# A language-model tower on one core: probabilities transposed during the last sequence, experts' tokens found in groups of three

## The reference

```python
combined = concat([_ngram_embed(byte_sequence, t, n) for t, n in zip(tables, (2, 3, 4))])
h = einsum('bsk,dk->bsd', combined, proj_w) + proj_b
# attention on layernorm(h): branches "cross" (keys from a stride-2 convolution), "dot" and "cosine",
# each softmax(q k^T) v and a layer norm; a 3-way softmax gate mixes the branches; h += z
x2 = layernorm(h)
Sm = softmax(x2 @ W_router + b_router)        # 8192 tokens x 32 experts
G, idx = top_k(Sm.T, 256)                     # each expert's 256 best tokens, ties to the lowest token
act = silu(x2[idx] @ W_up[group] + b_up)      # 4 experts share one W_up
y.at[idx].add(G * (act @ W_down[expert] + b_down))
return h + y
```

## Time and profile before

| | us |
|---|---|
| median of three runs | 1395.65 (1395.10 to 1399.89) |
| the profiled execution | 1398.12 |
| its span, first to last instruction | 1395.9 |
| PE / DVE / ACT / POOL busy | 1111.2 / 841.5 / 673.8 / 799.9 |
| first block | 0 to 1055.6 |
| threshold (30 steps) | 1060.5 to 1123.9 |
| masks and token lists until the first gather | 1123.95 to 1160.6 |
| first gather to first scatter | 1160.6 to 1187.0 |
| experts, first scatter to the end | 1187.0 to 1395.9 |

### The profile page before, as it was taken

One profiled execution on the slowest core, in us unless ns is written; L12 is line 12 of the kernel. 1 busy time (PEld: TensorE's weight loads), 2 busy tenths in 40 slices (PEclk: granted clock), 3 DMA queues, 4 the chain that ended last, 5 costly groups with the idle time before them and its releaser, 6 DMA issues. The chain is left out here.

```text
span 1395.9 us, 22815 instructions
## 1 busy us (share of the span) xinstructions
PE 1111.2 (80%) x7389; PEld 970.8 (70%) x7390; DVE 841.5 (60%) x2493; ACT 673.8 (48%) x1690; POOL 799.9 (57%) x1257
## 2 busy tenths in 40 slices
PE   4569999999999999999999999999953235666572
PEld 3459788888978878888887888788852124555462
DVE  4235677777676867767776777776756875111110
ACT  0335666656565655665565566555534515212110
POOL 5355676667467657747755864545550002788875
PEclk9979999999999999999999999999985556888877
DMA  2010000000001101001010100000001000444442
GB/s 93 16 29 20 16 26 29 22 26 27 9 24 29 30 13 39 24 9 30 23 30 22 31 22 9 17 11 9 18 17 51 0 0 19 78 80 82 82 75 28
DMA packets 49080, 42.45 MB, mean 30 GB/s; under 512 B 6728, under 2 KB 44488, under 8 KB 48840
## 3 DMA queue, kind: packets, MB, share of 16 engines
q0 software_dynamic: 18432, 22.04, 8.0%
q1 hardware_dynamic: 30536, 19.00, 4.5%
HBM read 27.38 MB, written 13.63 MB: 29 GB/s over the span
## 5 line engine op out<-in xcount | busy, mean ns | idle before, releaser
L595 PE MATMUL mixed<-v,pT 128*128 128x132 f32 x2560 | 324.5, 279 | 5.2 <-issue 4.8
L595 PEld LDWEIGHTS mixed<-v,pT 128*128 128x128 f32 x2560 | 307.3, 193 | 5.6 <-issue 5.6
L1046 POOL DMA_INDIRECT gram<-in_emb,ids x192 | 191.3, 997 | 75.0 <-issue 51.7
L827 DVE TENSOR_REDUCE neg_max<-scores 128x1 f32<-128x1024 f32 (+1 forms) x192 | 199.1, 1037 | 51.9 <-PE scores L408 50.0
L975 ACT ACTIVATE probs<-scores,neg_max 128x1024 f32<-128x1024 f32 (+1 forms) x192 | 186.5, 971 | 59.9 <-DVE neg_max L827 59.8
L984 ACT ACTIVATE pT<-turned 128x512 f32<-128x512 f32 x214 | 127.4, 595 | 65.4 <-PE turned L576 62.0
L576 PE MATMUL turned<-con,probs 128*128 128x128 f32 x856 | 128.0, 277 | 30.3 <-ACT probs L975 12.1
L1088 POOL TENSOR_TENSOR zb<-row,gate 128x384 f32<-128x384 f32 x64 | 54.6, 853 | 157.5 <-DVE gate L865 156.6
L406 PE MATMUL scores<-k_hi,q_hi 128*128 128x512 f32 x320 | 136.0, 425 | 1.9 <-DVE q_lo L730 1.9
L1650 POOL DMA_INDIRECT xg<-token_table,slots x64 | 63.8, 997 | 121.1 <-DVE slots L1533 101.9
L576 PEld LDWEIGHTS turned<-con,probs 128*128 128x128 f32 x856 | 99.3, 142 | 47.5 <-ACT probs L975 19.8
(11 more groups left out here) (335 smaller groups left out, 2422.1 us busy)
## 6 DMA issues: line engine op xcount, KB each, us to landing
wd<-in_w_down SPq DMA_DIRECT2D x32, 171.0 KB
token_table<-w SPq DMA_DIRECT2D x16, 320.0 KB
out_h<-h SPq DMA_DIRECT2D x16, 256.0 KB, 2.3
gram<-in_emb,ids POOLq DMA_INDIRECT x192
wu<-in_w_up SPq DMA_DIRECT2D x8, 170.5 KB
w<-in_weights SPq DMA_DIRECT2D x1, 1174.0 KB, 6.6
xg<-token_table,slots POOLq DMA_INDIRECT x64
out_h<-yw,slots POOLq DMA_INDIRECT x64
```

The lines of the kernel that those rows point to most:

```text
L595: last = pe.matmul(mixed[:, 0:VW], pT[:, n % 2, j * P:(j + 1) * P], vals, start=(j == 0), stop=(last_half and j == half * 4 + 3))
L827: dve.tensor_reduce(neg_max[:, n % 4:n % 4 + 1], scores[:, (n % 2) * S:(n % 2) * S + width], AX_X, ALU.max, negate=True).then_inc(maxed, 1)
L1046: pool.indirect_dma_start(gram[:, t % 4, g, :], None, emb[g], bass.IndirectOffsetOnAxis(ap=ids[:, s, t, g:g + 1], axis=0)).then_inc(gather ...
```

## The change

1. The shared banks are no longer handed out in turn: a small table of times (a unit is 4.9 long, users begin at 1.5, 2.2, 2.6 or 4.8 in it and hold a bank 2.7 or 1.7) picks the bank that comes free first.
2. In the last sequence the probabilities of the first six sequences are transposed as items in units 4, 6 and 8 (`probT0` to `probT2`, four blocks of four tiles each, one sequence being two blocks), those of the next three blocks in the tail (`probT3`); only the last block is transposed in the second block. The storage order of `prob` becomes that of the tiles.
3. The last tile is routed alone (`x2T2`, `route2`), the three ahead of it together. `prob` is written ahead of `trow`.
4. The stores to HBM are awaited by POOL ahead of its first gather, not by SP at the end of the first block. The bit tables are loaded in the first block.
5. The masks are made in four groups of eight experts. The rank of a tie is summed in PSUM by matmuls (`sums`, `places`) and compared with 256 in one DVE operation (`choose`), in place of the scan over all.
6. The token lists are found three experts at a time (`rank`, `rows_before`, `rows`, `reach`, `find_rows`). Two triples come before the first expert, the other nine stand inside the loop over experts, one in each of its first nine rounds.
7. For that the banks are divided anew: `up` has one bank pair and `down` one bank, no longer two by turns. Four experts are gathered ahead instead of three.

```diff
+UNIT_LONG = 4.9
+USED_AT = dict(first=1.5, half0=2.2, half1=2.6, second=4.8)
+HELD = dict(item=2.7, half=1.7)
...
-        _ring = (_ring + 1) % 3
+        _ring = min(range(3), key=lambda j: _free[j])
+        _start = max(_s * UNIT_LONG + USED_AT[_where], _free[_ring])
+        _free[_ring] = _start + HELD["item" if isinstance(_user, int) else "half"]
...
+LAST = tuple(line + extra for line, extra in zip(STEADY, ("",) * 4 + (" probT0", "", " probT1", "", " probT2") + ("",) * 15))
+DRAIN = ("|", "|", "|", "probT3- |", "|", "x2T1- |", "route1- |", "|", "x2T2- |", "route2- |")
...
-            for half in range(2):
-                sp.wait_ge(h1_stored[half], 16 * B)
-                sp.wait_ge(row_stored[half], 16 * B)
...
+            def probT_item(j, dst):
+                blocks = range(j * 4, min(j * 4 + 4, TT // CHUNKS - 1))
+                last_half = blocks[-1]
+                pe.wait_ge(route_v, (last_half + 1) * 5)
+                for i, u in enumerate(blocks):
+                    last = pe.transpose(dst[:, i * P:(i + 1) * P],
+                                        prob[:, u * CHUNKS:(u + 1) * CHUNKS, :].rearrange("p c e -> p (c e)"), ident)
...
-        for u in range(CT):
-            last = pe.transpose(scores[:, u * P:(u + 1) * P], prob[:, u * CHUNKS:(u + 1) * CHUNKS, :].rearrange("p c e -> p (c e)"), ident)
+        pe.transpose(scores[:, 0:P], prob[:, (CT - 1) * CHUNKS:CT * CHUNKS, :].rearrange("p c e -> p (c e)"), ident
+                     ).then_inc(prob_turned, 1)
...
+        def sums(g):
+            if g >= 1:
+                pe.wait_ge(sums_a, g)
+            pe.wait_ge(over_ok, g + 1)
+            for j in range(GE):
+                pe.matmul(down_bank[0:TT, j:j + 1], over[:, :, g * GE + j], ones_bf[:, 0:1], start=True, stop=True)
+            if g >= 2:
+                pe.wait_ge(chosen_ok, g - 1)
+            pe.matmul(place_bank(g), far_down[:], over[:, :, g * GE:(g + 1) * GE], start=True, stop=False)
+            pe.wait_ge(tie_ok, g + 1)
+            for j in range(GE):
+                last = pe.matmul(down_bank[0:TT, GE + j:GE + j + 1], tie[:, :, g * GE + j], ones_bf[:, 0:1],
+                                 start=True, stop=True)
+            last.then_inc(sums_t, 1)
+            pe.matmul(place_bank(g), upto_bf[:], tie[:, :, g * GE:(g + 1) * GE], start=False, stop=False)
+
+        def places(g):
+            pe.wait_ge(sums_a, g + 1)
+            pe.matmul(place_bank(g), ones_bf[0:TT, :], tile_sums[:, g, 0, :].unsqueeze(1).to_broadcast([TT, TT, GE]),
+                      start=False, stop=False)
+            pe.wait_ge(ties_ok, g + 1)
+            pe.matmul(place_bank(g), ones_bf[0:TT, :], ties_before[:, g, :, :], start=False, stop=True).then_inc(place_t, 1)
...
         def up(e):
             pe.wait_ge(xt_v, e + 1)
-            if e >= 2:
-                pe.wait_ge(hid_a, e - 1)
+            if e >= 1:
+                pe.wait_ge(hid_a, e)
...
         def down(e):
             pe.wait_ge(hid_a, e + 1)
-            if e >= 2:
-                pe.wait_ge(y_v, e - 1)
+            if e >= 1:
+                pe.wait_ge(y_v, e)
...
+        pe.wait_ge(chosen_ok, GROUPS)
         up(0)
         turn(1)
         for e in range(NE):
+            g = e + FIRST_TRIPLES
+            if g < len(TRIPLES):
+                rank(g)
             if e + 1 < NE:
                 up(e + 1)
+            if g < len(TRIPLES):
+                rows_before(g)
             down(e)
+            if g < len(TRIPLES):
+                rows(g)
             if e + 2 < NE:
                 turn(e + 2)
...
-        dve.tensor_scalar(thr_row[:], thr_row[:], cand[0:NE, :].bitcast(F32), None, ALU.add).then_inc(thr_v, 1)
-        everywhere = thr[:].unsqueeze(1).to_broadcast([P, CT, NE])
-        for mask, op in ((over, ALU.is_gt), (tie, ALU.is_equal)):
-            for c in range(CHUNKS):
-                last = dve.tensor_tensor(mask[:, c * CT:(c + 1) * CT, :], prob[:, c:TT:CHUNKS, :], everywhere, op)
...
-        dve.tensor_tensor_scan(tie_before[:].rearrange("p e t -> p (e t)"), keep[:].rearrange("p e t -> p (e t)"),
...
-        dve.tensor_tensor(chosen[:, 1:TT + 1, :], tie_in[:], over[:], ALU.add).then_inc(chosen_ok, 1)
...
+        def choose(g):
+            at = slice(g * GE, (g + 1) * GE)
+            if g == 0:
+                dve.wait_ge(made_g, 1)
+            dve.wait_ge(reach_ok, g + 1)
+            dve.wait_ge(place_t, g + 1)
+            dve.scalar_tensor_tensor(out=chosen[:, 1:TT + 1, at], in0=place_bank(g).rearrange("p (t e) -> p t e", e=GE),
+                                     scalar=float(TOPK), in1=reach_bf[:, :, at], op0=ALU.is_le, op1=ALU.mult
+                                     ).then_inc(chosen_ok, 1)
...
+        for kept in stored:
+            pool.wait_ge(kept, 16 * B)
         for e in range(AHEAD):
             gather(e)
```

More of the change, by code:

```diff
@@ L130, in v_done, with routed @@
     return V_COUNT[AT[item] + 1]
+def routed(s, j):
+    return range(*((0, 4), (4, 7 if s == B - 1 else 8), (7, 8))[j])
 def items_at(s):
@@ L768, in cos_scale, with route_logits @@
                                       ALU.mult).then_inc(qk_ready, 1)
-            def route_logits(k, s, half):
-                r = s * 2 + half
+            def route_logits(k, s, j):
+                r, m = s * 2 + j, len(routed(s, j))
                 dve.wait_ge(item_full, k + 1)
@@ L1359, in _ @@
-        for q in range(4):
-            last = pe.matmul(turned[:, 0:512], ones_bf[:], over[:, q * 16:(q + 1) * 16, :], start=(q == 0), stop=(q == 3))
-        last.then_inc(sums_t, 1)
-        pe.wait_ge(masks, 2)
-        pe.wait_ge(prob_copied, 4)
-        for q in range(4):
-            last = pe.matmul(scores[:, q * 512:(q + 1) * 512], ones_bf[:], tie[:, q * 16:(q + 1) * 16, :],
-                             start=True, stop=True)
-        last.then_inc(sums_t, 1)
-        pe.wait_ge(pick_v, 1)
@@ new lines, in rows_before, with rows @@
+        def rows_before(g):
+            e0, e1 = TRIPLES[g][0], TRIPLES[g][-1] + 1
+            pe.wait_ge(rank_a, g + 1)
+            pe.matmul(rank_bank[0:TT, 3 * P:3 * P + e1 - e0], below_bf[0:TT, 0:TT], ranks[:, e0:e1, P - 1],
+                      start=True, stop=True).then_inc(before_t, 1)
+        def rows(g):
+            pe.wait_ge(reached_ok, TRIPLES[g][-1] + 1)
+            for half in range(HALVES):
+                if g >= 1:
+                    pe.wait_ge((row_v, row_a)[half], g)
+                for i, e in enumerate(TRIPLES[g]):
+                    last = pe.matmul(row_bank(half)[:, i * RW:(i + 1) * RW], reached[:, e, half * P:(half + 1) * P],
+                                     ranks[:, e, :], start=True, stop=True)
+                last.then_inc(row_t, 1)
@@ L1430, in down @@
             last.then_inc(down_t, 1)
+        sums(0)
+        places(0)
+        rank(0)
+        rows_before(0)
+        rows(0)
+        rank(1)
+        sums(1)
+        rows_before(1)
+        rows(1)
+        places(1)
+        sums(2)
         pe.wait_ge(ones_set, 2)
         turn(0)
+        places(2)
+        sums(3)
+        places(3)
+        pe.wait_ge(chosen_ok, GROUPS)
         up(0)
@@ L1516, in _, with compare, find_over @@
-        dve.tensor_copy(before[:], scores[0:TT, 0:NE]).then_inc(before_v, 1)
-        dve.wait_ge(before_v, 1)
-        def reach(e0, e1):
-            for e in range(e0, min(e1, NE)):
+        dve.wait_ge(thr_v, 1)
+        def compare(mask, g, op):
+            at = slice(g * GE, (g + 1) * GE)
+            return dve.tensor_tensor(mask[:, :, at], prob[:, :, at], thr[:, at].unsqueeze(1).to_broadcast([P, TT, GE]), op)
+        def find_over(g):
+            compare(over, g, ALU.is_gt).then_inc(over_ok, 1)
@@ L1520, in reach @@
+        find_over(0)
+        find_ties(0)
+        find_over(1)
+        count_before(0)
+        choose(0)
+        find_ties(1)
+        def reach(g):
+            e0, e1 = TRIPLES[g][0], TRIPLES[g][-1] + 1
+            dve.wait_ge(before_t, g + 1)
+            dve.tensor_copy(before[:, e0:e1], rank_bank[0:TT, 3 * P:3 * P + e1 - e0]).then_inc(before_v, 1)
+            dve.wait_ge(before_v, g + 1)
+            for e in TRIPLES[g]:
                 dve.tensor_scalar(reached[:, e, :], slot_bf[0:TT, :], before[:, e:e + 1], None,
```

381 lines of the change are left out of this document (200 added, 181 removed).

## The result

The changed kernel takes **1350.15 us** (median of 4 runs, 1349.15 to 1351.42); beside it the kernel before took 1396.6 us (1395.1 to 1399.89). The ratio is 0.9665, 95% interval 0.9644 to 0.9685. 1358 was forecast. The profiled execution has a span of 1348.9 us, 47.0 less than before.

| stretch | before | after | change | forecast |
|---|---|---|---|---|
| first block, to the last output copied | 1034.62 | 1021.57 | -13.05 | -10 |
| from there to the second block on DVE | 21.00 | 19.52 | -1.48 | -4.6 |
| to the first count | 4.85 | 1.25 | -3.60 | -3.7 |
| search, to the first mask | 63.48 | 63.35 | -0.13 | 0 |
| first mask to first scatter | 63.02 | 33.75 | -29.27 | -26 |

What follows compares the result with a forecast made beforehand. PE was taken to bound the first block, POOL's gathers and scatters the expert loop, a chain between. Terms -10 -4.6 -3.7 -26 +8 -1 = -37.3 took 1398.12 to 1360.8; the median lying 2.5 lower, 1358 us, range 1350 to 1366.

Steps and rivals of the forecast that it cites:

- Banks: First block: the new table removes PE's bank waits, 2.0 us a sequence over six sequences, less 2 us for transposes: -10.
- the banks bring nothing: Rival for the first block: the bank waits just move to the next unit; 1368 us, chance 0.13.
- End of the first block: Last tile routed alone -3.2, later statistics +0.6, SP no longer awaiting the last store -2.0: sum -4.6 us.
- the +0.6 for the statistics: First block's end: DVE does three `route_logits` steps ahead of the last tile's statistics, ready some 0.6 us late.
- Start of the threshold: Before the first count: fewer transposes and no `thr_row`, about 1.5 us for 4.9: -3.7.
- Masks and lists: First mask to first scatter: the new order takes 37 us instead of 63: -26.
- The 3 us for long hops: Masks and lists: 3 us added to the 33.8 reckoned until the first scatter, since the hops were reckoned short.
- The loop: Loop over experts: nine rounds at 7.3 us against POOL's 6.43 give back +8; the fourth gather ahead gives -1.
- all goes well: Rival: the banks give 15 us and POOL covers the loop; 1345 us, chance 0.12.
- DVE holds POOL up: Rival in the loop: DVE's `reached` steps and list work delay POOL's issues, 17 us at most; 1368 us, chance 0.05.

Runs made afterwards that it cites:

- Runs 1: Changed kernel with the shared banks handed out in turn again: 1357.91 us, ratio 0.9769 to the kernel before.
- 2: Kernel before with only the new table of banks put in: 1378.89 us, ratio 0.9908 to the kernel before.
- Runs 3: Changed kernel with SP awaiting the landing of all stores at the first block's end again: 1345.29 us, ratio 0.9687 to the kernel before.
- 4: Changed kernel with the last four tiles routed together again: 1343.31 us, ratio 0.9673 to the kernel before.
- 12: Changed kernel with POOL making only the power for the last tile, DVE the shift, and five experts gathered ahead: 1331.21 us, ratio 0.9684.
- Run 5: Changed kernel with the six `up` matmuls made twice in each of the nine rounds with lists: 1343.34 us, ratio 0.9761 to the kernel before.
- run 9: Changed kernel with three added 512-column matmuls in each step of the threshold search: 1334.24 us, ratio 0.9697 to the kernel before.

## Why the prediction was right, and where it was not

**Banks**: right in mechanism and, a sequence, in size (2.06 us for 2.0). The sum was 3 us short (13.05 for 10). I had six sequences at 2 us less 2 us for the transposes of the probabilities, and nothing in the first two. The traces show 1.9 in the first two, 10.1 in the next four (2.5 each), 1.2 in the seventh and, up to the last output copied, a loss of 0.2 in the last. Runs 1 and 2 rule out "the banks bring nothing".

**End of the first block**: the step that failed. "One tile takes about 0.4 and 0.5" and the rest of it hold (5.9 us for 8.4), and so does the +0.6 for the statistics (+0.47). What failed is the sum of two savings on one wait, -4.6 where -1.5 was measured: I had SP and DVE as the only ones that end the block. POOL's DRAIN was in the trace before, ending 2.1 us ahead of SP; read from there, the most that all of it could give was those 2.1 us. Runs 3, 4 and 12 show it.

**Start of the threshold**: -3.60 for -3.7.

**Masks and lists**: -29.3 for -26. Each milestone but the last came a little late (11.9 for 10.8, 25.0 for 23.5), since a sum of eight columns takes 0.98 to 1.04 us for 0.9 to 1.0 and a 512-column matmul 0.61 for 0.45. I had spread the 1.9 us of a group over four where the clock was the same, but its mean of 623 ns was the number to take for one that stands alone. The 3 us for long hops were not needed, and `up(1)` took 1.81 us for 2.9.

**The loop**: mechanism right, size wrong, and the largest error of the sum: 7.3 us a round where 5.85 was measured, +0.7 where +7 was forecast. 6.9 was my path at full clock: with each step a little shorter than put (ACT's reductions 1.2 for 1.4) and the 0.4 of hops inside the steps, it is 1.0 less. And `up` took 1.52 to 1.55 us in seven of the nine rounds, 1.81 in the first and 2.76 in the eighth, so the 0.4 that I added for a slow clock was hardly needed. Run 5 shows the rule behind it: at 5.85 us, below POOL's 6.42, a round costs nothing, at 7.14 nine of them cost 7.8 us. The bound of the term (0, POOL covers all) is what happened, so the rival "all goes well" (1345) is nearer than the forecast: banks 13, loop 0.

**The sum**: the errors of the terms are -3.0 (banks), +3.1 (end of the block), +0.1 (start), -3.3 (lists) and -6.3 (loop), with the search and the end -9.7 in all. That banks and block end cancel is luck, and 1350.15 lies at the very edge of the 1350 to 1366 that I had given. A slip beside it: the bounds of the terms add up to some 1340 to 1398, not 1333 to 1399.

**DVE holds POOL up**: gathers beside DVE's masks take 0.95 to 1.45 us (1.29 for the first above), ten of them 10.8 us (the window from 1117.6 to 1139.4), at 0.95 each 9.5: 1.3 us at most, in POOL's idle time. In the loop a gather takes 1.02 or 0.98 us, before and after alike. The page "SBUF — State Buffer" of the Trainium skill, section "SBUF: two separate sides", names a mechanism that would stretch them; no run shows that it is the cause of those 1.3 us, and they cost nothing here.

## What to carry to other kernels

When two savings end in the same wait, list every engine's arrival there before adding them up: the next one to be late may be 2 us behind, and it may be a DRAIN that no busy row shows. Work put into this loop was free up to the pace of the engine that bounds it, and cost its whole excess beyond; so compare the round's path with that pace first, and the clock that it will have second. A table that assigns buffers by when they come free is worth what the waits at the wrong places are worth, and those can be read off a steady period, better off several: here the middle ones gave 2.1 to 2.9 us.

## What the runs showed of the hardware

POOL's DRAIN at the end of the first block took 7.43 us in every trace but the one where the last operation was the power (7.93); it ended 7.2 us behind the end of that operation. PE's took 0.48 to 1.91 us there, DVE's 0.33 to 0.53. At the end of the program POOL's took 4.8 or 4.95 us, and 3.5 in run 12. PE's granted clock stayed at 0.50 (1.2 GHz) through 45 us with PE busy for 39.25 (run 9). The same kernel reached its first count 18 us earlier on another chip, with later stages equal within 1.2 us; the stalls without a cause in the profile, one of 8.7 us on DVE among them, were absent there.
